# Attention with value products of 512 columns for all heads, and a context loaded in eight parts

## What is computed

```python
q = _split_heads(hidden_states @ q_w.T + q_b)
k = _split_heads(context @ k_w.T + k_b)          # context: 8 x 1601 x 512
v = _split_heads(context @ v_w.T + v_b)
scores = jnp.einsum('bhqd,bhkd->bhqk', q, k) / jnp.sqrt(jnp.float32(HD))
probs = jax.nn.softmax(jnp.where(mask, -jnp.inf, scores), axis=-1)
ctx = jnp.einsum('bhqk,bhkd->bhqd', probs, v)
```

## Time and profile before

| | |
|---|---|
| median of 3 runs | 1308.0 us (1307.15 to 1308.45) |
| the profiled execution | 1304.27 us, of which the span of its instructions is 1302.5 us |
| mean granted clock of PE | 0.984 of full speed |
| busy share | PE 96%, DVE 65%, ACT 52%, POOL 12% |
| chain that ended last, by engine | PE 93%, DVE 3%, ACT 1%, DMA 1% |

### The profile page before, as it was taken

One profiled execution on the slowest core, in us unless ns is written; L12 is line 12 of the kernel. 1 busy time (PEld: TensorE's weight loads), 2 busy tenths in 40 slices (PEclk: granted clock), 3 DMA queues, 4 the chain that ended last, 5 costly groups with the idle time before them and its releaser, 6 DMA issues.

```text
span 1302.5 us, 22157 instructions
## 1 busy us (share of the span) xinstructions
PE 1256.4 (96%) x8497; PEld 1170.1 (90%) x8497; DVE 840.5 (65%) x2183; ACT 675.3 (52%) x1194; POOL 156.9 (12%) x86
## 2 busy tenths in 40 slices
PE   6999999999999999999999999998779999999997
PEld 5799999999999999999999999997667988888986
DVE  4556656666566565656656556665756777877776
ACT  5345545534644454563554455345334667677673
POOL 2003101300400310130040021001040000000012
PEclk9999999999999999999999999999878999999999
DMA  7002200300220220031022013004216667676763
GB/s 286 27 1 90 79 2 15 126 28 1 90 79 2 86 83 1 2 114 53 2 90 79 1 32 121 1 1 154 85 40 231 219 227 258 226 242 238 233 213 109
DMA packets 61507, 129.05 MB, mean 99 GB/s; under 512 B 3572, under 2 KB 21120, under 8 KB 61160
## 3 DMA queue, kind: packets, MB, share of 16 engines
q1 hardware_dynamic: 59240, 120.85, 26.9%
q0 software_dynamic: 2176, 6.95, 1.6%
HBM read 121.89 MB, written 15.34 MB: 105 GB/s over the span
## 4 chain that ended last, share of the span: by engine, by line
PE 93%; DVE 3%; ACT 1%; DMA 1%; issue 1%; POOL 0%; SPq 0%; DVEq 0%; POOLq 0%
PE ptp L814 24%; PE work L814 21%; PE work L1090 8%; PE pv L929 7%; PE ptp L916 7%; PE work L852 6%; PE work L1092 4%; PE ptp L1111 2%; PE ptp L1112 2%; PE ptp L1114 2%; PE ptp L1113 2%; PE ptp L1115 2%; PE work L821 1%; DMA raw<-in_ctxT 1%; PE ptp L821 1%; DVE pt L1299 1%
## 5 line engine op out<-in xcount | busy, mean ns | idle before, releaser
L814 PE MATMUL ptp<-vw_hi,cx_hi 128*128 128x256 f32 x832 | 241.7, 291 | 0.0
L814 PE MATMUL ptp<-vw_lo,cx_hi 128*128 128x256 f32 x832 | 235.1, 283 | 0.0
L814 PE MATMUL ptp<-vw_hi,cx_lo 128*128 128x256 f32 x832 | 235.0, 282 | 0.0
L495 POOL TENSOR_TENSOR cx_lo<-raw,cx_hi 128x1664 fp32r<-128x1664 f32 x30 | 113.9, 3795 | 675.1 <-ACT cx_hi L555 675.1
L814 PE MATMUL work<-cx_hi,kw_hi 128*128 128x402 f32 x504 | 175.4, 348 | 1.7 <-POOL cx_lo L495 1.7
L814 PE MATMUL work<-cx_lo,kw_hi 128*128 128x402 f32 x504 | 174.5, 346 | 0.0
L814 PEld LDWEIGHTS ptp<-vw_hi,cx_hi 128*128 128x128 f32 x832 | 159.0, 191 | 16.9 <-issue 16.9
L814 PE MATMUL work<-cx_hi,kw_lo 128*128 128x402 f32 x504 | 173.8, 345 | 0.0
L1245 DVE SCALAR_TENSOR_TENSOR kk_lo<-work,biasT,kk_hi 128x402 fp32r<-128x402 f32 x128 | 79.6, 634 | 131.9 <-ACT kk_hi L568 131.4
L1299 DVE TENSOR_TENSOR pt<-ptp,pt 128x512 fp32r<-128x512 f32 (+1 forms) x224 | 141.5, 650 | 34.6 <-ACT pt L555 30.9
L814 PEld LDWEIGHTS ptp<-vw_lo,cx_hi 128*128 128x128 f32 x832 | 159.1, 191 | 0.0
(11 more groups left out here) (251 smaller groups left out, 2384.5 us busy)
## 6 DMA issues: line engine op xcount, KB each, us to landing
w1raw<-in_w SPq DMA_DIRECT2D x32, 1024.0 KB, 5.1
w2raw<-in_w SPq DMA_DIRECT2D x32, 1024.0 KB, 6.7
raw<-in_ctxT SPq DMA_DIRECT2D x31, 832.0 KB, 6.1
pr<-in_mask SPq DMA_DIRECT2D x8, 800.5 KB, 4.4
xrow<-x_rows SPq DMA_DIRECT2D x7, 256.0 KB, 6.0
y_rows<-y_out_rows POOLq DMA_DIRECT2D x7, 256.0 KB, 2.3
xin<-in_x SPq DMA_DIRECT2D x1, 1024.0 KB, 9.3
qwraw<-in_qwT SPq DMA_DIRECT2D x1, 1024.0 KB, 11.6
```

The source lines that it names most:

```text
L495: pool.tensor_tensor(cx[1][:, :, sl], raw[:, k % 2], cx[0][:, :, sl].bitcast(F32), ALU.subtract).then_inc(c_lo, 1)
L814: last = pe.matmul(dst, lhs(i, c), rhs(j, c), start=(c == 0 and (i, j) == (0, 0)), stop=(c == n - 1 and (i, j) == (1, 0)))
```

## The change

The values of all 16 heads are made once per batch: a `v` step is now one tile of context rows with 12 matmuls of 512 columns (`value_item`), 13 steps per batch where there were 14 of twice the matmuls. The last tile of context rows has 66 rows (`KEND`) where it was filled up to 128. The key chunks are 400 columns wide (the last one 402). The list of steps is written anew, since all values now lie in the first half of a batch. The context of the next batch comes in eight parts of 200 columns, at the steps that `NEXT_PARTS` names; the first batch has four buffers of its own (`raw0`). `turn_tokens` does its four transposes of 128 rows first and then those of 64. The memory for the descriptors of POOL's transfers is set to 4096.

```diff
-KC = 402
+TPH = KT // 2 + 1
+KC = 400
 NKC = 4
-LKP = KC * NKC
-CC = KP // NKC
+NCC = 2 * NKC
+CC = KC // 2
...
 def steps_of(last):
-        s = [[("s", 4 * h + 2 * i + rt, j) for j in (2 * u, 2 * u + 1) for rt in range(2)]
-             for i in range(2) for u in range(2)]
-        steps += s[0] + v[0:2] + s[1] + e[0:1] + v[2:3] + e[1:2] + v[3:4] + s[2] + v[4:6] + s[3] + e[2:3] + v[6:] + e[3:]
-        if k:
-            steps += k[:5] + t + k[5:6] + w[:1] + k[6:] + w[1:]
-        else:
-            steps += t + w
...
+    steps = s[0] + v[0:2] + s[1] + v[2:3] + e[0:1] + v[3:4] + e[1:2] + s[2] + v[4:6] + s[3] + v[6:7] + e[2:3]
+    steps += v[7:8] + e[3:4] + v[8:] + k[0][0:5] + t[0:1] + k[0][5:6] + w[0] + k[0][6:8]
+    steps += s[4] + w[1][0:3] + s[5] + w[1][3:]
+    if last:
+        return steps + e[4:6] + s[6] + s[7] + e[6:8] + t[1:2] + w[2] + w[3]
+    k = k[1]
+    steps += k[0:1] + e[4:5] + k[1:2] + e[5:6] + s[6] + k[2:4] + s[7] + k[4:5] + e[6:7] + k[5:6] + e[7:8] + k[6:8]
+    return steps + t[1:2] + w[2] + w[3]
...
+NEXT_PARTS = {("k", 1, 1): (0,), ("k", 1, 2): (1,), ("k", 1, 4): (2,), ("k", 1, 5): (3,), ("w", 0, 3): (4,),
+              ("k", 1, 6): (5,), ("k", 1, 7): (6,), ("w", 1, 2): (7,)}
...
-            def value_item(h, j, bank):
-                for n in range(min(2, KT - 2 * j)):
-                    kt = 2 * j + n
-                    last = products(bank[:, n * 2 * P:(n + 1) * 2 * P],
-                                    lambda i, c: cx[i][:, c, kt * P:(kt + 1) * P],
-                                    lambda i, c: vw[i][:, c, h * 2 * P:(h + 1) * 2 * P])
-                last.then_inc(w_full, 1)
+            def value_item(kt, bank):
+                rows = tile_rows(kt)
+                products(bank[0:rows, :], lambda i, c: cx[i][:, c, kt * P:kt * P + rows],
+                         lambda i, c: vw[i][:, c]).then_inc(w_full, 1)
...
-                for c in range(C):
-                    dst, cols = yb[2 + c // 2][:, (c % 2) * SLOTS:(c % 2 + 1) * SLOTS], slice(c * P, (c + 1) * P)
-                    pe.transpose(dst[:, 0:P], xrow[:, 0, cols], ident[:])
-                    last = pe.transpose(dst[:, P:SLOTS], xrow[0:TAIL, 1, cols], ident[0:TAIL, 0:TAIL])
-                    if c % 2:
-                        last.then_inc(xg_full, 1)
+                for st, rows in ((0, P), (1, TAIL)):
+                    for c in range(C):
+                        dst = yb[2 + c // 2][:, (c % 2) * SLOTS + st * P:(c % 2) * SLOTS + st * P + rows]
+                        last = pe.transpose(dst, xrow[0:rows, st, c * P:(c + 1) * P], ident[0:rows, 0:rows])
+                        if st and c % 2:
+                            last.then_inc(xg_full, 1)
...
-    nc = bacc.Bacc("TRN2", target_bir_lowering=False, num_devices=1)
+    nc = bacc.Bacc("TRN2", target_bir_lowering=False, num_devices=1, dynamic_dma_scratch_size=4096)
```

More of the change, by code:

```diff
@@ L365, in _, with load_part, load_first @@
         def _(sp):
[L366 to L371, removed]
+            def load_part(b, j):
+                if (b, j) > (1, 1):
+                    sp.wait_ge(c_lo, parts_done(b, j) - 1)
+                n = part(j).stop - CC * j
+                sp.dma_start(raw[:, j % 2, :, 0:n], ctxT[b:b + 1, :, part(j)].rearrange(
+                    "o (c p) n -> p (o c) n", p=P)).then_inc(ld_raw[j % 2], 16)
+            def load_first(k, cs, ready):
+                n = keys(k).stop - KC * k
+                sp.dma_start(raw0[:, k, cs, 0:n], ctxT[0:1, cs.start * P:cs.stop * P, keys(k)].rearrange(
+                    "o (c p) n -> p (o c) n", p=P)).then_inc(ready, 16)
             def load_mask(b):
@@ L403, in _ @@
             for b in range(LASTB):
-                for k in range(NKC):
-                    load_chunk(b + 1, k)
+                for j in range(NCC):
+                    load_part(b + 1, j)
                 first_rows(b)
@@ L499, in _ @@
             for k in range(2, NKC):
-                ctx_lo(0, k)
+                ctx_lo(raw0[:, k], keys(k), k + 1)
             for b in range(1, B):
-                for k in range(NKC):
-                    ctx_lo(b, k)
-            pool.wait_ge(c_lo, NKC * B)
+                for j in range(NCC):
+                    ctx_lo(raw[:, j % 2], part(j), parts_done(b, j) + 1)
+            pool.wait_ge(c_lo, parts_done(B, 0))
             pool.sem_inc(att_over, 1)
@@ L576, in kv_item @@
                 if kind == "k":
-                    key_hi(h, j, bank)
+                    key_hi(h, *key_at(h, j), bank)
                 else:
-                    n = min(2, KT - 2 * j)
-                    src = by_pair((ptp if spare(step) else work)[bank], n)
-                    dst = value_parts(vv, j, n)[0]
+                    src = by_pair(ptp[bank], j)
+                    dst = value_parts(vv, j)[0]
                     act.activation(dst[0], src[0], ACT.Copy)
@@ L652, in body @@
                         kv_item(b, last, step)
-                    if kind == "v" and a == 1 and j in LAST_READ and not last:
-                        ctx_hi(b + 1, LAST_READ[j])
                     if kind == "e":
                         exponentials(b, a)
-                    for j in turns(step):
-                        pt_item(b, j)
-                    if kind == "w":
+                    for i in turns(step):
+                        pt_item(b, i)
+                    if kind == "w" and j == TPH - 1:
                         fold(b, a)
+                    if not last:
+                        for i in NEXT_PARTS.get(step, ()):
+                            ctx_hi(b + 1, i)
             for b in range(LASTB):
@@ L851, in score_pair @@
                         rows = slice(2 * HD * rt, 2 * HD * (rt + 1))
-                        ins = pe.matmul(work[bank_of(last, both[rt])][:, 0:KC], qbd[i][rows, cc, :],
-                                        kk[j][rows, cc, k * KC:(k + 1) * KC], start=(i, j) == (0, 0), stop=(i, j) == (1, 0))
+                        ins = pe.matmul(wide(work[bank_of(last, both[rt])], k), qbd[i][rows, cc, :],
+                                        kk[j][rows, cc, keys(k)], start=(i, j) == (0, 0), stop=(i, j) == (1, 0))
                         if (i, j) == (1, 0):
@@ L880, in _ @@
                                 pe.wait_ge(ready[c // (C // 2)], 1)
-                        last = pe.matmul(work[m][:, 0:KC], kw[i][:, c, m * P:(m + 1) * P], cx[j][:, c, 0:KC],
+                        last = pe.matmul(wide(work[m], 0), kw[i][:, c, m * P:(m + 1) * P], cx[j][:, c, keys(0)],
                                          start=(c == 0 and (i, j) == PASSES[0]), stop=(c == C - 1 and (i, j) == PASSES[-1]))
```

193 lines of the change are left out of this document (100 added, 93 removed).

## The result

| | before | after |
|---|---|---|
| median | 1307.8 us (4 runs) | 1357.3 us (1356.6 to 1357.9, 4 runs) |
| span of the profiled execution | 1302.5 us | 1355.0 us |
| mean granted clock | 0.984 | 0.979 |
| ratio, 95% interval | | 1.0373 (1.036 to 1.0386) |

What follows compares the result with a forecast made beforehand. PE's matmul rate was taken as the bound in attention and experts. Gains of 21.8 us against losses of 58.3 us gave +36.5 us, median 1308.0 to 1344 us; range 1322 to 1360, main case 1328 to 1358.

Steps and rivals of the forecast that it cites:

- The rivals in which the waits stay away: Small attention waits absent, 1325 us, chance 0.16; key products drain in time, 1306 us, faster 0.06 or about equal 0.04.
- (1): Value products in attention: 2496 of 256 columns become 1248 of 512, saving 15.3 us.
- (2): Narrower key chunks: key products and score pair steps lose two columns each, saving 1.4 us.
- (3): Token transposes in seven experts: eight shape changes become two, 0.73 us less each, all gained, 5.1 us.
- (4): Scores right behind a key product wait for its bank: 0.87 us, 22 times, 19.1 us lost.
- (5): Fourth group right behind the third: first weighing waits for fold and adding, 2.31 us in seven batches, 16.2 us lost.
- (6): Third group's first weighing waits for DVE's low part of its turns: 0.9 us, seven times, 6.2 us lost.
- (7): Scores among second group's weighings: PE waits for DVE's low parts, 1.25 us in eight batches, 10.0 us lost.
- (8): Last batch, without values or keys behind the second group: PE waits 7.5 us, was 3.1; 4 us lost.
- (9): Context part 4's copy between `pt` copies in ACT's queue delays a weighing 0.4 us, seven times, 2.8 us lost.
- clock in seven batches: Rival: attention pauses drop the clock once per batch, 12 us more, 1356 us; chance 0.14 shared with two other cases.
- The lower bound "nothing" of the width: Value products save nothing if one of 512 columns takes twice the 0.1198 us of 256; time then 1359 us.

Runs made afterwards that it cites:

- run 1: Kernel before with only the new order of the transposes in `turn_tokens`: 1306.7 us, 0.9989.
- run 2: Changed kernel with one key product back before the third group's first weighing and two between third and fourth group: 1346.8 us, 1.0294.
- run 8: Changed kernel with the `xg` copies ahead of the last two parts of `h` on ACT and DVE: 1352.9 us, 1.0336.
- run 9: Kernel before with the new transposes and the `xg` copies ahead of the last two parts of `h`: 1303.7 us, 0.9964.
- run 5: Changed kernel with each value step issued as two halves of 256 columns into the same bank: 1362.7 us, 1.0417.
- run 6: Kernel before with rows of `cx` of 1666 in place of 1664 elements in memory: 1304.6 us, 0.9966.
- run 3: Changed kernel with the second half's score pairs one by one between key products and weighings: 1343.6 us, 1.0266.
- run 7: Changed kernel with ACT's copies of context part 3 and the parts behind it moved later: 1358.2 us, 1.0374.
- run 4: Changed kernel with score pairs one by one, key products back between last groups, last batch's pairs among second and third group's weighings: 1326.3 us, 1.0141.
- run 10: Changed kernel with second half relisted: score pairs two at a time behind weighings, keys between groups, context parts 3 to 7 moved: 1389.7 us, 1.0619.

## Why the prediction was right, and where its terms were off

Forecast 1344 us, measured 1357; the losses were seen, their places nearly all, and the sum was 13 us short. That is close to the upper end of the forecast's own band, 1328 to 1358; the band is also narrower than its words, since a third of 58.3 us is 19 us to either side. The rivals in which the waits stay away are ruled out by the waits shown above. Term by term, forecast and measured:

| term | forecast | measured | from |
|---|---|---|---|
| (1) values | -15.3 | -15.4 | 38.7 to 36.8 us per batch |
| (2) narrower chunks | -1.4 | -1.5 | keys 0.2 us per batch |
| (3) transposes | -5.1 | -1.4 | run 1 |
| (4) scores behind a key | +19.1 | +19.1 | 0.87 each, 22 times |
| (5) fourth behind third group | +16.2 | +14.2 | 2.03 each; run 2 |
| (6) third group's start | +6.2 | +6.8 | 0.97 each |
| (7) scores among weighings | +10.0 | +9.6 | 1.2 net each |
| (8) last batch | +4 | about +6.5 | below |
| (9) context's parts | +2.8 | +4.3 | 0.62 each |
| clock in seven batches | 0 (a rival) | about +5 | 3 falls |

The last batch took 110.0 us for 103.5. My terms for it were -1.9 - 0.2 + 0.9 + 1.25 + 4 = +4.0, so the missing 2.5 us are laid on (8). The measured column gives 47 us. Some 0.4 us per batch are in no term: the key products take 35.7 us in a batch of after and took 35.4, although the narrower columns save 0.2, because more of them stand beside scores, where the shape changes. With these the terms but (3) come to 51.5 us, where the starts show 45.2 + 6.5 = 51.7 for the batches. Outside them some 2 us are left beside (3); the descriptor memory, the first batch's own buffers and the eight parts in place of four have no run of their own.

**The step that failed is (3).** It said "PE has no other work to hide it, so it is all gained", because the windows showed PE at 290.0 of 295.0 us. Runs 1, 8 and 9 show a second bound of the same length, a ring of waits: PE's products, then ACT's and DVE's queues with the splits of the weights (`w_hi`, `w_lo`) and the copies of `h` and `xg`, then PE's next products. In an expert of after (1098 to 1140 us) the chain that ended last is 18% `w_hi` on ACT and 34% `w_lo` on DVE; in the same window of before and of run 8 it is all PE's. The transposes lie where this ring does not run over PE. PE was only just as long as the ring, so it showed no wait. In before the last copy of `xg` ends at 1095.26 us, and the first product that reads it starts 0.13 us later, which is also the distance in after (1109.39 and 1109.52), where PE does wait for it:

```profile
1094.71 0.55 DVE L1452 TENSOR_TENSOR xg<-pv,xg 128x384 fp32r<-128x384 f32 x1
...
1095.39 0.43 PE L1090 MATMUL work<-xg,w_hi 128*128 128x384 f32 x1
```

So what PE saved became wait: 0.71 us per expert. Its size was also off, 0.87 us for the forecast 0.73, which shows in the period of 37.6 us once the copies are earlier. Why ring and PE are alike to the hundredth no run shows.

**(1) was right in size by luck.** Only a third of it is the width. By runs 5 and 6 the width gives 5.7 us and the new row length of `cx` 3.7. The third part is four entries from other products into values per batch that no longer exist, 0.18 us each (5.93 - 48 x 0.1198), 5.8 us. No run has it alone, but it is what is left between two of them: all value products of a batch take 38.7 us before, 38.2 in run 6, 37.5 in run 5 and 36.8 in after, and between runs 6 and 5, with the same width and nearly the same rows, the entries are all that changes. This part is partly moved and not saved, since the scores now stand before keys and weighings. The Trainium skill (TensorE: Matmul & The Clock Gate, "Back-to-back issue gap") would by its rule for an isolated product give 2.5 ns per joined pair; 4.6 were measured in equal surroundings, so the page was nearer than my 12.3 ns, which compared products of two stages whose operands lie differently in memory. The lower bound "nothing" of the width and the 66 rows' 9 us did not come true; 66 rows cost nothing that shows.

**(4) to (7)** have their places as forecast, and their sizes within 2 us. Run 3 confirms (4) as a wait for the bank of the key product. Run 2 adds a condition to (6), and does not test it alone: the key product that it put behind the turns was taken from ahead of them, where it had kept the exponentials and the turns' copies apart in ACT's queue, and the wait grew.

**(9) was at another copy.** I put the wait behind part 4. In the trace of after it is the copy of part 3 that stands ahead of three copies of `pt` and holds them up (ACT's timeline):

```profile
218.52 0.60 ACT L612 ACTIVATE kk_hi<-work,biasT 128x400 fp32r<-128x400 f32 x1 [0.73 <-PE work L857]
219.01 0.86 ACT L596 ACTIVATE cx_hi<-raw 128x800 fp32r<-128x800 f32 x1
219.77 1.62 ACT L596 ACTIVATE pt<-ptp 128x512 fp32r<-128x512 f32 x3
```

Run 7 moved it and only moved the wait. It is 0.38 us in six of the seven batches and 0.67 in the one where the copy also waits 0.18 us for its transfer; by the starts a weighing there comes 0.62 us late.

**The clock** was a rival, put at every batch; it came in three of seven, in the one execution of after that was profiled. Windows around one fall of after; the wait of the fourth group ends at 502.83 us, and the clock is at 0.50 from 503.6 to 507.0:

```profile
503.50:504.40 0.90, 0.90 (x7) 0.90 (x6) 0.82 (x2) 0.17 (x1) 0.00 (x0) 0.56 1.03 345
504.40:507.70 3.30, 3.30 (x20) 3.30 (x19) 1.38 (x2) 1.30 (x3) 0.00 (x0) 0.60 0.05 15
507.70:511.00 3.30, 3.07 (x27) 2.47 (x25) 1.40 (x3) 1.46 (x4) 0.00 (x0) 1.00 0.00 0
```

Those batches take 116.8 us, 1.6 more than the others. Neither PE's steps nor its waits differ between a batch with the fall and one without. The last batch has the clock at 0.50 for 10.2 us in two stretches, where it had 3.4 us before; at half the rate that can account for the 2.5 us that (8) lacked, but no run has it apart. For it speaks that the wait of (8) itself was not underrated: it comes in two pieces of 3.4 us, the first for a bank that scores hold (`smx`), the second for `pt`, 6.8 us in all where the forecast had 7.5.

## What to carry to other kernels

An engine that is busy all the time is the bound only as far as the next ring of waits is shorter: before a saving on it is counted, follow that ring and ask which queue would be next. Here it was no shorter, and nothing was gained. A wait that is seen alone is a poor guide to a new order: in runs 2, 4, 7 and 10 moving steps cured one wait and made another, and the list found by adding up all in-order queues at once was the first to be faster than the kernel before. A step that empties a bank is badly placed behind one that waits for another engine's last result; in run 10 this made a wait of 2.7 us.

## What the runs showed of the hardware

Rows of 1664 elements (6656 bytes, a multiple of 512) for an operand that is loaded as the stationary one make products of 256 columns 0.120 us apart; rows of 1666 or 1602 make them 0.1175 to 0.118 us apart (runs 6 and 5). Products that stream the same memory show no difference (11.02 and 11.03 us for five).

A change between products of 128 and of 64 rows costs about 0.1 us on either side, also for products of 400 columns: in run 3 a pair takes 0.75 for 0.65 us, a key product 2.39 for 2.20 us. From 128 to 66 rows no such cost shows: the turn of the 66 rows takes 0.19 us in after (267.44 to 267.63) as that of the filled tile did before.

The granted clock fell to 0.50 for 3.4 us behind waits of no more than 2 us, in 3 of 7 batches of after, in 2 of 7 of run 3, and in none of run 5, whose waits in a batch are those of after within 0.3 us (one profiled execution of each). The Trainium skill (TensorE: Matmul & The Clock Gate, "Why this matters for your kernels") advises against pauses of more than about 3 us; here the clock fell behind shorter ones, several of them in a batch. What decides between a batch with a fall and one without stays open.
